# A two-layer block with retention: the retention product in three rounded terms from the fifth tile on, and a new order of work in the first stage

## What is computed

```python
mod = (_silu(L0_c) @ L0_wmod).reshape(16, 6, 1, -1)
sa, ca, ga, sb, cb, gb = (mod[:, n] for n in range(6))
h = _layernorm(x) * (1 + ca) + sa
sig = sigmoid(h @ W_ret + b_ret)
ret = scan over tokens: xi = 0.5 * sig_t + 0.5 * xi
h = _layernorm(h + ret, ln1_scale, ln1_bias)
ffn = gelu(h @ W1 + b1) @ W2 + b2          # 256 -> 1024 -> 256
x = x + ga * _layernorm(h + ffn, ln2_scale, ln2_bias)
h = _layernorm(x) * (1 + cb) + sb          # goes on to a router and 16 experts
```

## Time and profile before

| what | value |
|---|---|
| time, median of 3 runs | 3453.37 us (3452.68 to 3454.29) |
| profiled execution, its own time | 3452.36 us |
| its span | 3450.5 us |
| mean granted clock of TensorE | 0.984 of full speed |
| PE busy | 3308.2 us, 96% of the span |
| DVE busy | 2609.4 us, 76% |
| ACT busy | 2076.5 us, 60% |
| POOL busy | 1272.1 us, 37% |
| mean DMA rate over the span | 106 GB/s |

### The profile page before, as it was taken

The page is one execution under the profiler, slowest core; times in us unless marked ns, Lnnn a source line. Parts: engine busy times, 40 slices in busy tenths (PEclk is TensorE's granted clock), DMA queues, the critical chain, the costliest instruction groups (busy, mean ns, idle before and its releaser), DMA issues.

```text
span 3450.5 us, 67723 instructions
## 1 busy us (share of the span) xinstructions
PE 3308.2 (96%) x25221; PEld 2796.1 (81%) x25221; DVE 2609.4 (76%) x6178; ACT 2076.5 (60%) x4056; POOL 1272.1 (37%) x1076
## 2 busy tenths in 40 slices
PE   6999999999998999999999479999999999999999
PEld 4888888888887799999999357888888888888888
DVE  5877887788778865555554578888888888888884
ACT  4677777777765556565665345555555555555554
POOL 1333333332332366666664432233333333232320
PEclk8999999999999999999999689999999999999999
DMA  4332233212212444444443465555555555565541
GB/s 181 103 115 93 90 115 109 78 67 81 75 45 80 97 118 95 106 95 107 106 106 76 91 128 122 124 121 118 127 130 124 128 119 124 128 130 125 127 103 41
DMA packets 746053, 366.38 MB, mean 106 GB/s; under 512 B 551310, under 2 KB 696278, under 8 KB 745590
## 3 DMA queue, kind: packets, MB, share of 16 engines
q1 hardware_dynamic: 717246, 319.55, 36.7%
q0 software_dynamic: 28416, 42.49, 6.7%
q10 hardware_dynamic: 64, 0.02, 0.0%
HBM read 224.93 MB, written 135.99 MB: 105 GB/s over the span
## 4 chain that ended last, share of the span: by engine, by line
PE 86%; DVE 6%; ACT 2%; DMA 2%; issue 1%; POOL 1%; SPq 1%; PEldq 0%; PEld 0%; DVEq 0%; ACTq 0%; POOLq 0%
PE bank L1015 10%; PE bank L1813 10%; PE bank L1797 10%; PE bank L2495 10%; PE bank L2509 10%; PE bank L994 10%; PE bank L2466 6%; PE bank L130 5%; PE bank L971 3%; PE bank L2445 3%; PE bank L2477 2%; PE bank L2440 1%; ACT sides L1343 1%; PE bank L979 1%; PE bank L1007 1%
## 5 line engine op out<-in xcount | busy, mean ns | idle before, releaser
L1686 DVE TENSOR_TENSOR hidden_low<-bank,hidden_high 128x512 fp32r<-128x512 f32 x256 | 176.3, 689 | 262.2 <-ACT hidden_high L1396 261.9
L641 ACT ACTIVATE bank<-bank,b 128x512 f32<-128x512 f32 x256 | 172.6, 674 | 279.3 <-PE bank L994 279.0
L1389 ACT ACTIVATE bank<-bank,fc_bias 128x512 f32<-128x512 f32 x256 | 169.5, 662 | 263.2 <-PE bank L1797 263.2
L2253 ACT ACTIVATE bank<-bank,l_b 128x512 f32<-128x512 f32 x256 | 168.9, 660 | 238.6 <-PE bank L2495 238.4
L1015 PE MATMUL bank<-w_high,gT_low 128*128 128x256 f32 x1024 | 309.7, 302 | 2.9 <-DVE gT_low L782 2.9
L2509 PE MATMUL bank<-l_w_high,l_hidden_low 128*128 128x256 f32 x1024 | 307.6, 300 | 0.0
L2466 PE MATMUL bank<-bandT,window 128*32 128x96 f32 x5632 | 271.8, 345 | 22.3 <-DMA bandT<-bands 20.1
L1015 PE MATMUL bank<-w_high,gT_high 128*128 128x256 f32 x1024 | 289.3, 283 | 0.0
L1015 PE MATMUL bank<-w_low,gT_high 128*128 128x256 f32 x1024 | 289.3, 283 | 0.0
L2509 PE MATMUL bank<-l_w_low,l_hidden_high 128*128 128x256 f32 x1024 | 286.0, 279 | 0.0
L2509 PE MATMUL bank<-l_w_high,l_hidden_high 128*128 128x256 f32 x1024 | 285.6, 279 | 0.0
(11 more groups left out here) (402 smaller groups left out, 10718.8 us busy)
## 6 DMA issues: line engine op xcount, KB each, us to landing
bandT<-bands SPq DMA_DIRECT2D x352, 240.0 KB, 3.6
fc_full<-in_L_ffn_fc_wT SPq DMA_DIRECT2D x32, 1024.0 KB, 5.7
bands<-zeros SPq DMA_DIRECT2D x22, 768.0 KB, 8.3
x<-in_L_attn_x SPq DMA_DIRECT2D x32, 512.0 KB, 6.2
moe_output<-zeros SPq DMA_DIRECT2D x32, 512.0 KB, 7.1
moe<-moe_output SPq DMA_DIRECT2D x32, 512.0 KB, 6.9
x_after_retention<-x SPq DMA_DIRECT2D x31, 512.0 KB, 2.8
moe_input_and_gates<-xn SPq DMA_DIRECT2D x31, 512.0 KB, 7.7
```

The costliest lines, as they stand in the source:

```text
L641: e.activation(bank[:, :], bank[:, :], ACT.Gelu_apprx_tanh, bias=t.b1[:, f:f + 1]).then_inc(s("g_full"), 1)
L1686: v.tensor_tensor(t.hidden.low[:, n % SLICES, :], K.banks[t.bank["expand", i, f, 0]][:, :], t.hidden.high[:, n % SLICES, :], ALU.subtract) ...
```

## The change

Four things change, all in the first stage.

1. From tile 4 on (`SPLIT_FROM`), `w_ret` and `h1T` are held in two parts, and each half of the retention product is six matmuls of fp32r operands in place of two of fp32. ACT makes the high part of `h1T` (`retain_high`, two copies of 128x512 a tile), POOL the low part (`retain_low`, two subtractions). The parts of `w_ret` are made once (`take_ret`). They lie where the conditions' weights were.
2. SP issues no zeros in the first four tiles (`ZEROS_FROM`). The four are made up with tile 8; the bands' zeros go from tile 4 to tile 25.
3. The conditions' products 1 to 5 come behind the first tile's turn of `r`.
4. The tables of places and banks have new numbers, and `FIRST_B` shifts the steps of tiles 0 to 2 one by one (`course_b` sorts the steps with these shifts).

```diff
-EARLIER = {"l1_mlp0": ("mlp_in0", 16), ...
+EARLIER = {"h1_high": ("b_weights", 192), "h1_low": ("vectors", 64), "l1_mlp0": ("mlp_in0", 16), ...
 PLACES_B = {
-    "split": 32.61, "low": 33.17, "contract": 34.97, "load": 0.05, "stats_in": 4.27, "root_in": 10.64, "norm_in": 10.08,
-    "modulate": 14.7, "retain": (18.28, 20.14), "run": (21.91, 21.91), "norm_mid": 26.41, "stats_mid": 27.91, "root_mid": 29.06,
+    "split": 32.93, "low": 33.35, "contract": 34.91, "load": 1.92, "stats_in": 8.09, "root_in": 9.31, "norm_in": 10.27,
+    "modulate": 15.11, "retain_high": 15.5, "retain_low": 15.56, "retain": (18.7, 20.69), "run": (21.9, 22.19), "norm_mid": 26.36,
...
-ONCE_B = [(20.6, "mod_products"), (22.0, "mod_copies"), (22.3, "take_mlp", 0), (30.9, "fields"), ...
+ONCE_B = [(26.65, "take_mlp", 0), (27.49, "mod_products"), (27.55, "mod_copies"), (27.9, "fields"), ...
+          (38.37, "gain", 1, 5), (40.08, "rows", 1), (40.97, "take_ret")]
+SPLIT_FROM = 4
+ZEROS_FROM = 4
+FIRST_B = {("add_row", 0): 0.02, ... ("run", 0): -6.91, ("run", 1): -0.45, ... ("stats_in", 0): 3.89, ("stats_in", 1): -0.61, ...
...
 # SP
-            e.dma_start(moe_dram[i], t.zeros[:, 0:t.C * K.D]).then_inc(s("zeros_sent"), 16)
-            if i < 2 * K.NT:
+            if i >= ZEROS_FROM:
+                for n in ([*range(ZEROS_FROM), i] if i == 2 * ZEROS_FROM else [i]):
+                    e.dma_start(moe_dram[n], t.zeros[:, 0:t.C * K.D]).then_inc(s("zeros_sent"), 16)
+                n = i - ZEROS_FROM
+                if n < 2 * K.NT:
...
 # POOL
+        elif name == "take_ret" and i == 0:
+            e.wait_ge(*K.setup("scalar", "ret_high"))
+            e.tensor_tensor(t.ret_split.low[:, :, :], t.w_ret[:, :, :], t.ret_split.high[:, :, :], ALU.subtract)...
+        elif name == "retain_low" and i >= SPLIT_FROM:
+            for k in range(K.KD):
+                n = K.KD * (i - SPLIT_FROM) + k
+                e.wait_ge(*K.later("h1_high", n + 1))
+                e.tensor_tensor(t.h1_split.low[:, k, :], t.h1T[:, k, :], t.h1_split.high[:, k, :], ALU.subtract)...
 # ACT
+        elif name == "take_ret" and i == 0:
+            e.wait_ge(s("rows_sent"), 32)
+            e.copy(t.ret_split.high[:, :, :], t.w_ret[:, :, :]).then_inc(s("scalar_setup"), 1)
+        elif name == "retain_high" and i >= SPLIT_FROM:
+            for k in range(KD):
+                e.wait_ge(s("h1T"), 2 * i + k + 1)
+                e.copy(t.h1_split.high[:, k, :], t.h1T[:, k, :]).then_inc(K.later("h1_high")[0], 1)
 # PE
-            for j in range(KD):
-                m = pe.matmul(bank[:, :], t.w_ret[:, j, k * P:(k + 1) * P], t.h1T[:, j, :], start=j == 0, stop=j == KD - 1)
+            if i < SPLIT_FROM:
+                for j in range(KD):
+                    m = pe.matmul(bank[:, :], t.w_ret[:, j, k * P:(k + 1) * P], t.h1T[:, j, :], start=j == 0, stop=j == KD - 1)
+            else:
+                if k == 0:
+                    pe.wait_ge(*K.setup("pool", "ret_low"))
+                    pe.wait_ge(*K.later("h1_low", KD * (i - SPLIT_FROM + 1)))
+                for j in range(KD):
+                    for n, (w, x) in enumerate(t.ret_split[:, j, k * P:(k + 1) * P].pairs(t.h1_split[:, j, :])):
+                        m = pe.matmul(bank[:, :], w, x, start=j + n == 0, stop=j == KD - 1 and n == 2)
```

More of the change, by code:

```diff
@@ L352 @@
 BANKS_B = {
[L353 to L354 removed]
+    "modulate": (2, 3.49), "norm_mid": (2, 7.77), "affine_mid": (2, 4.51), "retain": (1, 3.39), "turn_out": (2, 1.6),
+    "route": (1, 0.27), "expand": (1, 5.43),
 }
@@ L363, in evenly, with course_b @@
 def evenly(count, steps, slices):
-    return [(place + slices * i, name, i, *args) for place, name, _, *args in steps for i in range(count)]
+    return [(place + slices * i + FIRST_B.get((name, i), 0.0), name, i, *args) for place, name, _, *args in steps for i in range(count)]
+def course_b(count, placed):
+    slices = sum(name == "expand" for _, name, *_ in placed)
+    timed = [(place + slices * i + FIRST_B.get((name, i), 0.0), n, name, i, *args) for n, (place, name, _, *args) in enumerate(placed) for i in range(count)]
+    return [step for _, _, *step in sorted(timed, key=lambda z: z[:2])]
 def timed_banks(steps, wanted, of, paired=()):
@@ L410, in retention_tiles @@
     t.sumsq = K.ring(ctx, "sumsq", 2, [P, C])
-    placed = order_b(KF)
-    t.steps, t.bank = [step for _, *step in placed], timed_banks(evenly(t.N, placed, KF), BANKS_B, range(6))
+    t.placed = order_b(KF)
+    t.bank = timed_banks(evenly(t.N, t.placed, KF), BANKS_B, range(6))
     return t
@@ L430, in later_retention_tiles @@
     t.x1, t.h2, t.xn = (K.ring(ctx, n, 2, [P, C, D]) for n in ("x1_", "h2_", "xn"))
+    t.ret_split, t.h1_split = K.split_tile(ctx, "w_ret", [P, K.KD, D]), K.split_tile(ctx, "h1T", [P, K.KD, t.GT])
     t.xnT = K.tile(ctx, "xnT", [P, C, D])
@@ L468, in retention_sync @@
     e.wait_ge(*K.setup("pool", "zeros"))
-    for name, i, *args in ordered(t.N, t.steps):
+    for name, i, *args in course_b(t.N, t.placed):
         if name == "load":
@@ L558, in retention_pool @@
             root("rms", "var_rms", i)
+        elif name == "take_ret" and i == 0:
+            e.wait_ge(*K.setup("scalar", "ret_high"))
+            e.tensor_tensor(t.ret_split.low[:, :, :], t.w_ret[:, :, :], t.ret_split.high[:, :, :], ALU.subtract).then_inc(s("pool_setup"), 1)
+        elif name == "retain_low" and i >= SPLIT_FROM:
+            for k in range(K.KD):
+                n = K.KD * (i - SPLIT_FROM) + k
+                e.wait_ge(*K.later("h1_high", n + 1))
+                e.tensor_tensor(t.h1_split.low[:, k, :], t.h1T[:, k, :], t.h1_split.high[:, k, :], ALU.subtract).then_inc(K.later("h1_low")[0], 1)
         elif name == "affine_mid":
```

40 lines of the change are left out of this document (30 added, 10 removed).

## The result

The changed kernel takes 3533.39 us (median of 4 runs, 3532.67 to 3536.07) against 3453.02 us for the kernel before on the same chip (3451.22 to 3454.29): a ratio of 1.0235, 95% interval 1.0217 to 1.0252. It is slower by 80 us, where 17 less were predicted: 3436 us, in a range from 3428 to 3444. The prediction gave "slower", its rival C, a chance of 0.04. Its profiled execution took 3533.74 us with a span of 3531.9.

What follows compares the result with a forecast made beforehand. PE was taken as the bound, busy all of a full tile. 3452.36 - 17.9 (product) + 1.4 (late `gT_low`) - 1 (start) = 3434.9; with 1.0 for the median 3435.9, rounded to 3436 us, range 3428 to 3444.

Steps and rivals of the forecast that it cites:

- rival C: DVE waits for POOL's new subtractions at `xn`, `stats_in`, `gT_low`: 2.6 us, PE 1.0 a tile, 3462 us; chance 0.04.
- The product: PE's retention half falls from 1.71 to 1.39 us, saving 0.64 a tile, 17.9 us over 28 tiles.
- rival A2: A term streams at 0.214 us a matmul in place of 0.232, saving 0.43 a half: 3430 us; chance 0.02.
- What is late next: `gT_low` behind DVE's `stats_out` loses its 0.30 us slack: 0.05 a tile, +1.4 us, ends 0 and +8.
- The added work on ACT: Two copies a tile, 1.35 us in all; the last slice's `gT_low` still ends 1.6 us early: no cost.
- The added work on POOL: Two subtractions, 2.6 us a tile; only `root_in` queued behind, POOL has 20 us of idle a tile: no cost.
- The place of `xn`: On DVE, `xn`, then `stats_in`, then the last slice's `gT_low`, with 1.6 us of slack.
- The start: First expansion at 58 us, where it was 58.27; DVE's stall for tile 2's `x` goes: -1 us, from -3.5 to +3.

Runs made afterwards that it cites:

- old_places_split: The kernel before, with its places, banks, zeros and start, plus the three-term split product from tile 4 on: 3445.31 us, ratio 0.9956.
- adds_only: `old_places_split` with the added ACT copies, POOL subtractions and PE's waits kept, but the product itself in fp32: 3452.11 us, ratio 0.9999.
- no_split: The changed kernel with the retention product in fp32 on all tiles, without ACT's copies and POOL's subtractions (`SPLIT_FROM` 32): 3483.22 us, ratio 1.0067.
- xn_beside: `old_places_split` with `rms_norm` (`xn`) at 47.9 in place of 49.08, beside POOL's work: 3440.77 us, ratio 0.9964.
- stats_behind: The changed kernel with `stats_in` at 8.5 in place of 8.09, behind the last slice's `gT_low`: 3478.05 us, ratio 1.0073.
- stats_late: `old_places_split` with `stats_x1` at 42.2 in place of 42.12, behind the `gT_low` that PE waits for: 3443.41 us, ratio 0.9974.
- zeros_and_xn: `old_places_split` with the zeros from tile 4 on (`ZEROS_FROM` 4) and `rms_norm` at 47.9: 3439.08 us, ratio 0.9956.
- xn_later: The changed kernel with `rms_norm` (`xn`) at 49.3 in place of 47.9, behind `stats_in` and the last `gT_low`: 3448.91 us, ratio 0.9963.
- low_memset: The changed kernel with POOL's subtractions replaced by memsets of zeros, so the product lacks its term with `h1T_low`: 3467.38 us, ratio 1.0025.

## Why the prediction was wrong

**The product: right.** Three terms take a half from 1.71 to 1.38 (forecast 1.39), 0.33 saved of the forecast 0.32. The rival A2, with the count of passes of the Trainium skill (FP8 and Floating Point Precision, TensorE Precision Notes), did not come: the twelve matmuls of a tile are 0.23 apart, not 0.214.

**What is late next: right in kind, mis-sized.** I took 0.05 a tile for the `gT_low` behind `stats_out`, with ends 0 and 0.3. In the old order the tile misses the forecast by 0.16 (`old_places_split`), 4.5 us where 1.4 stood in the sum. That a late `gT_low` is the cause is likely and not shown.

**The added work on ACT: right.** `adds_only` finds nothing, and DVE waits for `gT_high` less in the changed kernel (65.1 us between 62 and 1040) than in the one before (105.5).

**The added work on POOL: the step that failed.** The prediction costs it with "nothing" since POOL has 20 us of idle a tile, and holds its neighbour DVE for undisturbed. It names the mechanism in rival C and sets it aside with the sentence "the pair above cost 0.45, not microseconds". That 0.45 was a mean over sixteen records, 592 against 481 ns. Their extremes and starts would have said something else. In a tile of before three `xn` are undisturbed, and the first takes 0.95: it begins at 868.10, while the row's addition runs, and the next begins at 868.97, 0.24 after POOL went on to `root_in`. It took 0.95 because 0.67 of the addition was left when it began: it ended 0.28 after it, as the waiting `xn` of the changed kernel do. Elsewhere in the stage one took 2.01. This is a lock held for what remains of the other's instruction, not a slowdown in proportion. Behind the addition there was only `root_in`, which held no `xn` (the second and third follow within 0.47 of each other):

```profile
866.37 2.40 POOL L567 TENSOR_TENSOR x<-x,rows_v 128x1024 f32<-128x1024 f32 x1
868.73 1.20 POOL L536 TENSOR_TENSOR root_in<-var_in,minus_half 128x4 f32<-128x4 f32 x1
```
```profile
868.10 0.95 DVE L828 SCALAR_TENSOR_TENSOR xn<-h,root_rms,nw_row 128x256 f32<-128x256 f32 x1
...
868.97 0.87 DVE L828 SCALAR_TENSOR_TENSOR xn<-h,root_rms,nw_row 128x256 f32<-128x256 f32 x2
```

The price of a place is then the number of large POOL readers still to end there, each for its length or what is left of it: one remainder before, two in `no_split` (`hT_low` and the addition, 4.57 for the four), four with `h1T_low` (6.65), against 1.9 undisturbed. Rival C had 2.6 us of waiting, for the new subtractions alone. It is 4.7, as `hT_low` and the addition hold `xn` too, once it begins among them: of the 4.5 us by which the four `xn` grew (2.14 to 6.65), 2.4 came with the new places (`no_split`) and 2.1 with the subtractions. The Trainium skill, SBUF — State Buffer, "Who interferes with whom", calls what these two engines share an exclusive lock and names this pair, a DVE instruction with two SBUF inputs and a POOL instruction that reads SBUF, as one that contends. The traces here agree; the prediction cited it and let a mean outweigh it.

**The place of `xn`: second half of the same step.** The prediction set no price on the move of `rms_norm` from 49.08 to 47.9 and of `stats_in` to just behind it, ahead of the `gT_low` that PE waits for. It had read this from the order (C names the row of work), and gave it 1.6 us of slack from laid-out durations, all of them undisturbed ones. `xn_beside` and `stats_behind` show that this queue decides: waits of `xn` cost nothing in the one, and 1.3 less than in the changed kernel in the other.

**The lower clock: not foreseen.** 0.6 a tile, or 16 us, came from TensorE's clock after the pauses of 2.6 us. Rival C would have been too cheap by that as well: it had 1.0 us of waiting a tile and 3462 us; the chip had 2.6, the clock and 3533.

**The start: right, and not by luck.** First expansion forecast at 58, measured 57.81, and the steps on the way came as laid out: the second `th` done at 26.09 (forecast 26), `r` at 28.07 (28.5), tile 1's `xh` at 33.61 (34.1). But the gain of the late zeros was given away in the new start: with the old places they bring it to 53.73. The start is not equally long in kernels with the same start: the first expansion begins anywhere from 56.34 (`old_places_split`) to 58.65 (`stats_late`) with the zeros as before, and at 53.73 and 55.40 (`zeros_and_xn`) with late ones; the gain is some 3 us on average, of the 6 by which DVE's stall shrinks. It is too small for the ratios.

## What to carry to other kernels

Where DVE operations with two SBUF inputs and POOL's readers meet, count how many large POOL instructions are still to end at that spot; each may hold one DVE operation for its whole length. Read the shortest, median and longest of the DVE operation, since a mean hides a lock. An idle engine does not make added work on it free: ask what it holds while it runs, and what is queued behind the operation that is held. A pause of some microseconds in a saturated TensorE can also cost clock behind it.

## What the runs showed of the hardware

- A DVE operation of 0.47 us with two SBUF inputs took up to 2.64 us beside a POOL tensor operation, ended 0.27 to 0.29 us after that one did, and its successor then waited for the next POOL instruction: one for one. POOL's instruction behind was 0.18 us longer (1.47 against 1.29). `gT_low`, with one input in SBUF and one in PSUM, was not held (0.69 us).
- It also goes the other way. When DVE's subtraction of `w_low` (two SBUF inputs, 128x2048) ran first, POOL's `root_mid` on 128x4 elements, 1.01 us by itself in the kernel before, took 2.98, in every run with the new places. `xn_later`:

```profile
40.60 2.28 DVE L803 TENSOR_TENSOR w_low<-L_attn_W,w_high 128x2048 fp32r<-128x2048 f32 x1
40.77 2.98 POOL L572 TENSOR_TENSOR root_mid<-var_mid,minus_half 128x4 f32<-128x4 f32 x1 [4.44 <-DVE var_mid L762]
```

- POOL's memset of 128x1024 (1.0 us), which reads nothing, held no `xn` (`low_memset`), though it ran at the same place.
- A tiny POOL operation is lengthened but doesn't hold: `root_in` on 128x4 elements takes 1.02 us alone and 1.20 beside `xn` (rows above), whose own records stay at 0.47 beside it.
- With PE pausing 2.6 us a tile the granted clock fell for one stretch in nearly every second tile (0.98 on average, 0.58 over the 3.4 us shown), and the twelve matmuls behind a pause took 1.70 us at full clock, 2.93 otherwise, in place of 1.44; with waits of at most 1.3 us (`stats_behind`) it did not fall between 400 and 700 us.
